# Small products of a graph network kernel, cut to 64 and 32 stationary columns

## What is computed

```python
h = relu(layernorm(x))                      # over 1024, no weight, no bias
x = x + attention(h)                        # q,k,v, inner q,k,v, output: 7 matrices of 1024 x 1024
h = relu(layernorm(x))
out = h @ root + bias
for r in range(8):
    mask = (edge_type == r)
    sums = segment_sum(h[src] * mask[:, None], dst)
    cnt = segment_sum(mask, dst)
    out = out + (sums / maximum(cnt, 1)[:, None]) @ weight[r]
z = concatenate([out, h], 1) @ w_gate + b_gate
x = x + tanh(out) * z + h * (1 - z)
```

## Time and profile before

| what | value |
|---|---|
| three runs | 227.9, 228.2, 230.13 us, median 228.2 |
| profiled execution | 227.98 us, span 225.8 us |
| PE, PEld busy | 216.0 us (96%), 210.1 us (93%) |
| DVE, ACT, POOL busy | 80.6, 22.3, 23.2 us |
| granted TensorE clock | full speed in all slices of the span |
| read from memory | 75.97 MB |

### The profile page before, as it was taken

One profiled execution on the slowest core, in us unless ns is written; L12 is line 12 of the kernel. 1 busy time (PEld: TensorE's weight loads), 2 busy tenths in 40 slices (PEclk: granted clock), 3 DMA queues, 4 the chain that ended last, 5 costly groups with the idle time before them and its releaser, 6 DMA issues.

```text
span 225.8 us, 10194 instructions
## 1 busy us (share of the span) xinstructions
PE 216.0 (96%) x4797; PEld 210.1 (93%) x4797; DVE 80.6 (36%) x138; ACT 22.3 (10%) x41; POOL 23.2 (10%) x53
## 2 busy tenths in 40 slices
PE   2999998998999999999999999999999999999994
PEld 2889988998999999898999999999999999999993
DVE  2479638050399930555738500000000000000624
ACT  2550000000020110132033000000000000000101
POOL 2271005500000000010000940000000000000000
PEclk9999999999999999999999999999999999999999
DMA  6999999999999999999999799999999999998002
GB/s 225 366 393 422 421 422 421 380 376 385 363 386 385 328 383 376 363 359 399 412 360 379 209 306 398 328 383 388 398 380 361 369 350 338 356 363 332 6 3 70
DMA packets 14684, 77.01 MB, mean 341 GB/s; under 512 B 4874, under 2 KB 5138, under 8 KB 5428
## 3 DMA queue, kind: packets, MB, share of 16 engines
q1 hardware_dynamic: 14112, 75.96, 88.5%
q10 hardware_dynamic: 532, 0.42, 0.6%
HBM read 75.97 MB, written 0.39 MB: 338 GB/s over the span
## 4 chain that ended last, share of the span: by engine, by line
PE 95%; DMA 2%; issue 1%; DVE 1%; ACT 0%
PE acc L780 81%; PE acc L1027 4%; DMA x_sb<-in_x 2%; PE turn L968 1%; PE side L828 1%; PE side L968 1%; PE side L1027 1%; PE turn L856 1%; DVE stats L505 1%; PE acc L798 1%; PE turn L798 0%; PE turn L872 0%; PE side L839 0%; PE turn L839 0%; PE acc L872 0%
## 5 line engine op out<-in xcount | busy, mean ns | idle before, releaser
L780 PE MATMUL acc<-mean,raw 128*64 128x96 f32 x2048 | 84.7, 246 | 0.0
L780 PEld LDWEIGHTS acc<-mean,raw 128*64 128x64 f32 x2048 | 84.6, 137 | 0.0
L780 PE MATMUL acc<-hT,raw 128*64 128x96 f32 x1024 | 44.4, 247 | 0.3 <-issue 0.3
L780 PEld LDWEIGHTS acc<-hT,raw 128*64 128x64 f32 x1024 | 42.9, 137 | 1.4 <-issue 1.1
L743 DVE TENSOR_TENSOR uT<-acc,uT 128x384 f32<-128x384 f32 x2 | 1.1, 558 | 80.9 <-PE acc L780 80.9
L780 PE MATMUL acc<-kT,raw 128*64 128x96 f32 x512 | 22.1, 246 | 0.8 <-issue 0.8
L780 PEld LDWEIGHTS acc<-kT,raw 128*64 128x64 f32 x512 | 21.5, 137 | 1.3 <-issue 1.2
L780 PE MATMUL acc<-qT,raw 128*64 128x96 f32 x512 | 22.0, 246 | 0.7 <-issue 0.7
L780 PEld LDWEIGHTS acc<-qT,raw 128*64 128x64 f32 x512 | 21.4, 137 | 1.0 <-issue 1.0
L780 PE MATMUL acc<-uT,raw 128*64 128x96 f32 x256 | 12.6, 266 | 0.0
L780 PEld LDWEIGHTS acc<-uT,raw 128*64 128x64 f32 x256 | 12.2, 152 | 0.3 <-ACT uT L409 0.2
(11 more groups left out here) (177 smaller groups left out, 148.3 us busy)
## 6 DMA issues: line engine op xcount, KB each, us to landing
raw<-in_weights SPq DMA_DIRECT2D x284, 256.0 KB, 4.7
raw<-in_weights SPq DMA_DIRECT2D x1, 1024.0 KB, 5.9
x_sb<-in_x SPq DMA_DIRECT2D x1, 192.0 KB, 3.5
x_sb<-in_x ACTq DMA_DIRECT2D x1, 192.0 KB, 3.7
out<-out_rows SPq DMA_DIRECT2D x1, 192.0 KB, 2.1
out<-out_rows ACTq DMA_DIRECT2D x1, 144.0 KB, 2.4
out<-out_rows SPq DMA_DIRECT2D x1, 48.0 KB, 2.2
bias_rows<-in_biases ACTq DMA_DIRECT2D x1, 36.0 KB
```

What stands on the lines that cost most here:

```text
L780: mm = pe.matmul(a[g * HD:(g + 1) * HD, b, c * N:(c + 1) * N], raw[:, s, at:at + HD], moving(k0 + k), start=opens and k0 == 0 and c == 0 a ...
```

## The change

Six edits. The constant `ones` of 128 x 128 in F32R gives way to `ones_h` of 96 x 64 in F16. ScalarE writes a second copy of the counts, `counts_h` in F16, ahead of the F32R one, under a new semaphore `counts_halved`. The two scales, the totals, the variance and the 16 counts are each split into two products: the scales and totals into two halves of 64 stationary columns (128 partitions written), the variance and the counts, which write 96 partitions, into `NODES`, a part of 64 columns and one of 32. The totals wait for `counts_halved` in place of `counts_taken`, and multiply F16 by F16.

```diff
+        counts_h = sb("counts_h", [N, R * N], F16)
-        ones = sb("ones", [P, P], F32R)
+        ones_h = sb("ones_h", [N, HD], F16)
+        counts_halved = sem("counts_halved")
+        NODES = [slice(0, HD), slice(HD, N)]
-            gp.memset(ones[:, :].bitcast(F32), 1.0).then_inc(consts_ready, 1)
+            gp.memset(ones_h[:, :], 1.0).then_inc(consts_ready, 1)
             act.wait_ge(counts_split, 1)
+            act.activation(half(counts_h, 0), packed_low[:, :], ACT.Copy).then_inc(counts_halved, 1)
+            act.wait_ge(counts_split, 2)
+            act.activation(half(counts_h, 1), packed_high[:, :], ACT.Copy, scale=1.0 / PACK).then_inc(counts_halved, 1)
             act.activation(half(counts, 0), packed_low[:, :], ACT.Copy).then_inc(counts_taken, 1)
-            act.wait_ge(counts_split, 2)
             act.activation(half(counts, 1), packed_high[:, :], ACT.Copy, scale=1.0 / PACK).then_inc(counts_taken, 1)
...
+            def spread_diagonal(to, diag):
+
+                for g in range(2):
+                    mm = pe.matmul(to[g * HD:(g + 1) * HD, :], ones_f[:, 0:HD], diag[:, :], start=True, stop=True)
+                return mm
...
-                pe.matmul(side[0:N, 0, 0:TW], src_hot[:, c, :], rel_hot[:, c, :], start=c == 0,
-                          stop=c == EC - 1).then_inc(counted, 1)
+                for part in NODES:
+                    mm = pe.matmul(side[part, 0, 0:TW], src_hot[:, c, part], rel_hot[:, c, :], start=c == 0,
+                                   stop=c == EC - 1)
+                mm.then_inc(counted, 1)
...
-            pe.matmul(acc[1][:, 0, 0:N], ones_f[:, :], scale_diag[:, :], start=True, stop=True).then_inc(scale_shown, 1)
+            spread_diagonal(acc[1][:, 0, 0:N], scale_diag).then_inc(scale_shown, 1)
...
-            pe.matmul(turn[0:N, 1, 0:1], chunk_sum[:, 3, :], inv_width[:, 0:1], start=True,
-                      stop=True).then_inc(var_shown, 1)
+            for part in NODES:
+                mm = pe.matmul(turn[part, 1, 0:1], chunk_sum[:, 3, part], inv_width[:, 0:1], start=True, stop=True)
+            mm.then_inc(var_shown, 1)
...
-            pe.matmul(turn[:, 1, 0:N], ones_f[:, :], x1_diag[:, :], start=True, stop=True).then_inc(x1_scale_shown, 1)
-            pe.wait_ge(counts_taken, 2)
-            for b in range(2):
-                mm = pe.matmul(bank(side, b), ones[0:N, :], half(counts, b), start=True, stop=True)
+            spread_diagonal(turn[:, 1, 0:N], x1_diag).then_inc(x1_scale_shown, 1)
+            pe.wait_ge(counts_halved, 2)
+            for b in range(2):
+                for g in range(2):
+                    mm = pe.matmul(side[g * HD:(g + 1) * HD, b, 0:TW], ones_h[:, :], half(counts_h, b), start=True,
+                                   stop=True)
             mm.then_inc(totals_shown, 1)
```

## The result

The changed kernel takes 233.61 us (median of 6 runs, 231.92 to 234.35) against 228.49 us before (6 runs, 227.0 to 230.13). The ratio is 1.0227 with a 95% interval of 1.018 to 1.0274: slower by 5.1 us, well clear of no change; whether by more than 2% is left open by the interval. The profiled execution took 234.06 us with a span of 231.6 us, 5.8 us more than the span of before.

What follows compares the result with a forecast made beforehand. The prediction took TensorE's own work to bound the kernel, busy for 96% of the span. Its terms, 5.74 - 0.225 - 0.425 + 0, gave +5.1 us and 233.3 us, range 229.5 to 235.0 us.

Steps and rivals of the forecast that it cites:

- Size classes: On TensorE, a change of the size to which rows and columns round up costs some 0.11 to 0.145 us; 32 its own.
- two-row product: Product of 2 contraction rows ahead of the layer-0 scale, which takes 0.39 us; read as a size apart from 96 rows.
- Counts, +5.74 us: Counts at line 828: 30 changes and 32 products one after another, 8.89 us in place of 3.15 us.
- The 0.114 us a change: Price of a size change into a count's part on TensorE, estimated at 0.114 us, bounds 0.094 to 0.145 us.
- Scale of layer 0, -0.225 us: Line 883: four matmuls as in the pieces, following pieces free; 0.31 us in place of 0.535 us.
- Scale of layer 1 and totals, -0.425 us: Lines 982 and 985: F16 pairs run two abreast, 0.49 us in place of 0.915 us; the bound saves 0.10 us.
- Variance, 0: Line 978: split into 64 and 32 columns, nothing gained or lost; bounds -0.1 to +0.1 us.
- ScalarE, GpSimd, the late `average`, 0: Two added copies (1.04 us), a smaller memset and a second `average` 0.9 us later all stay hidden: no cost.
- The ring: Weight transfers into slots: memory is ahead of TensorE, so no transfer wait takes over; a slower TensorE fills the slots.
- Rival B: In counts and variance, 32 columns behave as 64, with no emptying between them: 1.5 us less, 226.7 us; chance 0.10.
- SyncE's waits for slots: Sign on SyncE: its waits for slots, 7.9 us before, grow by about as much as the 5 us shift.
- the long stretch of pieces: Sign in the chain: the stretch from 121 us on keeps its length and moves by 5 us.

Runs made afterwards that it cites:

- counts_33: Changed kernel with the second part of each count 33 columns wide in place of 32; ratio to the kernel before 0.9959.
- variance_rows64: Changed kernel with the counts' second part widened to 64 columns and the variance summing only 64 of 128 features; executed once, 226.08 us.
- the padded kernels: Changed kernel with the counts' second part widened to 64 columns: counts alone 231.9 us (one execution), variance widened too, ratio to the kernel before 0.9986.
- counts_whole: Changed kernel with counts and variance again one product of 96 columns each, halved scales and totals kept; ratio to the kernel before 0.9977.
- counts_thirds: Changed kernel with each count in three parts of 32 columns in place of 64 and 32; ratio to the kernel before 0.9993.
- counts_padded: Changed kernel with only the counts' second part widened from 32 to 64 columns, variance left at 64 and 32; executed once, 231.9 us.
- codes_padded: Changed kernel with second parts of counts and variance widened to 64 columns and the 16 edge-code products as pairs of 64; ratio 0.9978.

## Why the prediction was right

Forecast 233.3 us, measured 233.61 us; forecast +5.1 us, measured +5.1 us between the medians. That the totals agree to 0.3 us is partly luck: they scatter by several microseconds, and the interval of the ratio alone spans +4.1 to +6.3 us. What speaks for the mechanism is that each term below was met; they add up to some +5.0 us.

- *Size classes.* That the columns round up to 32, 64 or 128 and that a change costs had as nearest row a two-row product that also changed type. `counts_33` shows it for columns (32 are a size, 33 go with 64), and `variance_rows64` shows for rows that 64 and 128 differ; that FP32 and F16 of one size follow each other free is in the chain after (0.17, 0.33, 2.64 us). The Trainium skill, "TensorEngine Tiling (Array Packing)", "Key Properties", says that a change of the tiling mode drains TensorE; these traces agree, with the 0.11 us a change that the page doesn't give.
- *Counts, +5.74 us.* Measured: 1.52 + 6.98 us and two changes of 0.15 us are 8.8 us against 3.15 us, +5.65 us. The 0.114 us a change, which took the load of 96 columns out of a measured 0.134 us, was met: 0.108 to 0.114 us. So two things make the loss: 32 products one behind another need 2.6 us more than 16, and the changes some 3.3 us.
- *Scale of layer 0, -0.225 us.* 0.32 us and no delay behind it, -0.22 us. *Scale of layer 1 and totals, -0.425 us:* -0.42 us; the F16 pairs run abreast.
- *Variance, 0.* 0.21 us and the piece's delay, against 0.26 us and the same: -0.05 us.
- *ScalarE, GpSimd, the late `average`, 0.* Nothing of them is in the chain. The ring kept PE supplied: none of its waits is put down to a transfer of weights.
- *Rival B* did not occur, but its arithmetic for parts of one size was right up to one term: the padded kernels showed a wait of 0.2 us on VectorE ahead of the second `average`, which B's sum of -1.5 us had left out.

Two of the signs that the prediction named came out only in part. SyncE's waits for slots were to grow by about as much as the loss; they went from 7.9 to 11.2 us, by 3.3 us:

```profile
SPq L310 <- PE acc L788: 11.2, 12, 6.0
```

And the long stretch of pieces was to keep its length and move by 5 us. It starts 4.5 us later (125.44 us) and is 1.24 us longer (91.21 us with its pause, against 89.97 us), 0.99 us of it the pause.

## What to carry to other kernels

Before a product is cut, write down the size class of each product in the order in which TensorE runs them, and count the changes between neighbours: in this kernel each is 0.11 to 0.15 us, and unequal classes also don't overlap. The classes shown here are, for columns, 32 alone, 33 and 64 together, and 96 apart from these; for rows, 64 apart from 128, and 96 together with 128. That the bounds lie at 32 and 64 for rows too, and that 65 columns go with 96, was not tried. Cut to the class of the neighbours (64 and 64, or three times 32, took 2.6 and 2.8 us for the counts where 64 and 32 took 8.5 us), and widen a remainder into that class if the further outputs harm nobody; or sort the products by class. And read the cost of a stretch of a few microseconds from the chain: the totals here could not resolve 1 us.

## What the runs showed beyond that

The totals of one kernel scatter by 2 to 3% (before: 226.03 to 231.99 us in 29 runs), and the profiles show two places where. The first piece, 64 matmuls right behind the first ReLU, took 3.70 us (`counts_whole`) to 5.11 us (`counts_thirds`), with no edit near it. The table by microsecond shows two rates in it: 16 matmuls a microsecond at first, 62 ns each against the bare 41.3 ns, until it turns faster at a moment that differs, between 9 and 10 us in `counts_whole` and after 11 us in the kernel before. The granted clock is shown as full in all of it:

```profile
8.00:9.00 1.00, 1.00 (x16) 1.00 (x16) 0.29 (x1) 1.00 (x2) 0.00 (x0) 1.00 0.89 335
11.00:12.00 1.00, 1.00 (x28) 1.00 (x24) 0.00 (x0) 0.00 (x0) 0.41 (x2) 1.00 0.89 328
```

(These are rows of the kernel before: window, PE, PEld, VectorE, ScalarE and GpSimd busy us with counts, clock, DMA share, GB/s.) And pauses inside pieces that the trace gives no releaser, such as this one in the kernel after:

```profile
189.19 0.99 issue
```

were 1.8 us together before, 2.1 us after, 0.8 us in `counts_thirds` and 3.5 us in `counts_padded`, added up along the chain. What causes either is open. I tried nothing on it.

Narrow F16 products overlap more than I had rows for: three of 32 columns run abreast, and a load with its matmul every 21 ns was reached in `codes_padded`.
